# Cross-attention and FFN, one core: the add of head outputs and residual moves from VectorE to GpSimd

## The reference

```
q, k = layernorm(x), context
scores = (q k^T / 8 + hop products(q, rpe[hops])) * decay(gates)     # causal
h      = scores v / (normalizer + 1e-6)
hn     = headwise_layernorm(h) * (1 + ln_w) + ln_b
x1     = x + hn                                                      # the sum that is moved
n      = layernorm(x1)
out    = x1 + n base_w^T + base_b + 2 * (top-2 router mix of n lora_A) lora_B
```

## The kernel before, in words

| table | steps of t = 0, 1, 2, 3 | what is done |
|---|---|---|
| `SCALE` | 1, 4, 7, 10 | POOL: x_res += ln_b (L670), att_w = att * head_rs (L675), att_w *= 1 + ln_w (L680) |
| `LAYER` | 2, 5, 8, 11 | DVE: x1 = att_w + x_res (L1140), bn_stats (L1143), bn_aggr (L1146) |
| `TURN` | 3, 6, 9, 12 | ACT: rstd (L701, L703); DVE: norm (L1115); PE: transposes (L1225); POOL: x1_b = x1 + base_b (L665) |
| `ROUTE` | 4, 7, 10, 13 | PE: L1357; DVE: the router, twelve small instructions from L1077 to L1102 (`mix`) |
| `BASE` | 5, 8, 11, 14 | PE: transpose of mix (L1330), base product (L1344, L1346) |
| `OUT` | 6, 9, 12, 15 | DVE: out = x1_b + product (L1062); SPq: store |

## Time and profile before

### The profile page before, as it was taken

How to read it: one execution, slowest core, us unless ns; L and a number is a source line. 1 busy time by engine, 2 the same in 40 slices (tenths; PEclk the granted TensorE clock), 3 DMA queues, 4 the chain that set the end, 5 groups by cost and what they waited for, 6 DMA issues and landing times.

```text
span 4462.6 us, 82557 instructions
## 1 busy us (share of the span) xinstructions
PE 3690.6 (83%) x21556; PEld 2143.2 (48%) x21556; DVE 2695.9 (60%) x5561; ACT 1925.9 (43%) x4449; POOL 2188.5 (49%) x2567
## 2 busy tenths in 40 slices
PE   6777878878777877688889888888888888988897
PEld 4555544444444444345445444444444444544443
DVE  4545444444344444377777777777676776777774
ACT  3544444444344434354444444444444444444442
POOL 4567667777677777233333333333333333333332
PEclk9999989999999999799999999999999999999999
DMA  7889989999899999554344344444444434444341
GB/s 219 271 263 304 301 275 313 314 312 313 269 311 316 312 312 313 205 175 143 129 161 151 140 141 134 161 144 137 152 135 157 143 127 162 138 156 135 130 154 47
DMA packets 400329, 912.17 MB, mean 204 GB/s; under 512 B 54234, under 2 KB 152538, under 8 KB 391924
## 3 DMA queue, kind: packets, MB, share of 16 engines
q1 hardware_dynamic: 297716, 574.59, 37.5%
q0 software_dynamic: 102400, 335.63, 23.9%
HBM read 708.17 MB, written 201.85 MB: 204 GB/s over the span
## 4 chain that ended last, share of the span: by engine, by line
PE 31%; DVE 17%; issue 7%; ACT 2%; DVEq 1%; DMA 1%; ACTq 0%; SPq 0%; POOL 0%
PE psum L1344 7%; PE psum L1280 5%; PE psum L1288 5%; PE psum L1225 4%; PE psum L1304 3%; PE psum L1258 3%; DVE arena L1011 2%; PE psum L1346 2%; DVE arena L1019 1%; PE psum L1357 1%; DVE arena L1087 1%; DVE arena L991 1%; DVE arena L1082 1%; DVE arena L998 1%; DVE arena L1021 1%
## 5 line engine op out<-in xcount | busy, mean ns | idle before, releaser
L634 POOL DMA_INDIRECT arena<-in_L_xattn_rpe_dram,arena x1280 | 1220.0, 953 | 512.1 <-issue 305.7
L1200 PE MATMUL psum<-arena 128*128 128x128 f32 x5120 | 743.2, 287 | 350.2 <-DMA arena<-in_L_xattn_rpe_dram,arena 169.0
L1200 PEld LDWEIGHTS psum<-arena 128*128 128x128 f32 x5120 | 564.8, 145 | 632.7 <-DVE arena L471 241.3
L471 DVE COPY arena<-psum 128x512 f32<-128x512 f32 x640 | 442.6, 692 | 399.3 <-PE psum L1200 395.9
L471 ACT COPY arena<-psum 128x512 f32<-128x512 f32 x640 | 376.2, 588 | 644.2 <-PE psum L1200 643.8
L1211 PE MATMUL psum<-arena 128*64 128x128 f32 (+3 forms) x4096 | 649.3, 449 | 2.9 <-DVE arena L471 2.2
L654 POOL TENSOR_SCALAR_AFFINE_SELECT arena<-arena 128x256 f32<-128x256 f32 x256 | 113.4, 443 | 1033.2 <-ACT arena L779 1029.7
L479 DVE COPY arena<-psum 128x128 f32<-128x128 f32 (+3 forms) x512 | 251.3, 491 | 536.6 <-PE psum L1211 530.3
L1225 PE MATMUL psum<-arena 128*128 128x128 f32 x2176 | 346.6, 294 | 241.9 <-ACT arena L756 118.5
L779 ACT ACTIVATE arena<-arena 128x512 f32<-128x512 f32 (+3 forms) x1024 | 503.7, 557 | 54.3 <-issue 51.2
L1011 DVE TENSOR_TENSOR arena<-psum,arena 128x1024 f32<-128x1024 f32 (+1 forms) x384 | 400.6, 1043 | 183.9 <-PE psum L1288 159.0
(11 more groups left out here) (100 smaller groups left out, 4427.6 us busy)
## 6 DMA issues: line engine op xcount, KB each, us to landing
hop_products<-arena SPq DMA_DIRECT2D x64, 1024.0 KB, 6.2
arena<-in_x_dram SPq DMA_DIRECT2D x256, 256.0 KB, 4.0
arena<-gate_rows SPq DMA_DIRECT2D x128, 512.0 KB, 3.8
arena<-hop_products SPq DMA_DIRECT2D x128, 512.0 KB, 5.6
hop_products<-arena SPq DMA_DIRECT2D x64, 768.0 KB, 5.4
arena<-hop_products SPq DMA_DIRECT2D x128, 384.0 KB, 4.4
arena<-in_x_dram SPq DMA_DIRECT2D x512, 64.0 KB
hop_products<-arena SPq DMA_DIRECT2D x64, 512.0 KB, 4.7
```

The lines of the kernel that those rows point to most:

```text
L471: copy(rowsT[v % 2][:, :, o[2] * P:(o[2] + 1) * P], bank(1 + n % 2).rearrange("p (k m) -> p k m", k=KT)).then_inc(stage.sem, stage.step(o))
L634: nc.gpsimd.indirect_dma_start(out=rows[v][:, t, :], out_offset=None, in_=rpe[:, :], in_offset=bass.IndirectOffsetOnAxis(ap=here[:, t, v:v ...
L1200: last = nc.tensor.transpose(bank(1 + n % 2)[:, q * P:(q + 1) * P], rows[v][:, o[2], q * P:(q + 1) * P], ident)
```

## The change

The add `x1 = att_w + x_res` is taken from DVE's `LAYER` step and put on POOL behind the scaling of the same tile, one step earlier. The waits that spoke of DVE's x1 now speak of POOL's; DVE's bn_stats waits for POOL's x1. POOL's new instruction waits for its own L680 and for the norm (L1115) of two tiles before, which reads the same buffer of x1.

```diff
@@ steps of the semaphores @@
             for t in at_step(LAYER, s):
-                dve_f_steps[part] += [(n, t) for n in ("x1", "stats", "mean")]
+                dve_f_steps[part] += [(n, t) for n in ("stats", "mean")]
             for t in at_step(SCALE, s):
-                pool_f_steps[part] += [(n, t) for n in ("x_b", "scale", "weight")]
+                pool_f_steps[part] += [(n, t) for n in ("x_b", "scale", "weight", "x1")]
@@ SyncE, load_residual @@
-                sp.wait_ge(*dve_f.at(r.b, ("x1", (t - 2) % ST), 1 if t < 2 else 0))
+                sp.wait_ge(*pool_f.at(r.b, ("x1", (t - 2) % ST), 1 if t < 2 else 0))
@@ GpSimd, x1_b @@
-                        pool.wait_ge(*dve_f.at(r.b, ("x1", t)))
+                        pool.wait_ge(*pool_f.at(r.b, ("x1", t)))
@@ GpSimd, SCALE @@
-                            pool.wait_ge(*dve_f.at(rf.b, ("x1", (t - 1) % ST), 1 if t < 1 else 0))
+                            pool.wait_ge(*pool_f.at(rf.b, ("x1", (t - 1) % ST), 1 if t < 1 else 0))
...
                             nc.gpsimd.tensor_tensor(flat, flat, ln_w1, ALU.mult).then_inc(*pool_f.inc(("weight", t)))
+                            pool.wait_ge(*pool_f.at(rf.b, ("weight", t)))
+                            pool.wait_ge(*dve_f.at(rf.b, ("norm", (t - 2) % ST), 1 if t < 2 else 0))
+                            nc.gpsimd.tensor_tensor(x1[t % 2], flat, x_res[t % 2], ALU.add).then_inc(
+                                *pool_f.inc(("x1", t)))
@@ VectorE, LAYER @@
-                        dve.wait_ge(*pool_f.at(r.b, ("weight", t)))
-                        dve.wait_ge(*pool_f.at(r.b, ("x1_b", (t - 2) % ST), 1 if t < 2 else 0))
-                        nc.vector.tensor_tensor(x1[i], att_w.rearrange("p h d -> p (h d)"), x_res[i],
-                                                ALU.add).then_inc(*dve_f.inc(("x1", t)))
-                        dve.wait_ge(*dve_f.at(r.b, ("x1", t)))
+                        dve.wait_ge(*pool_f.at(r.b, ("x1", t)))
                         nc.vector.bn_stats(f_stats[:, 0:6], x1[i]).then_inc(*dve_f.inc(("stats", t)))
```

## The result

The changed kernel takes 4551.91 us (median of 4 runs, 4543.33 to 4565.5), the one before 4463.36 (4 runs); the ratio is 1.0192 (95% interval 1.0166 to 1.0218). Forecast were 4511 us and a range up to 4548: the direction was right, the size was not. The profiled executions have spans of 4462.6 and 4541.6 us, 79 us apart, all of it in the second stage; the medians are 88.5 us apart, and the profiled execution is the fastest of the four of the changed kernel, which range over 22 us. In many of the executions further down, of the kernel before too, the first stage took 2312 to 2376 us instead of 1819, so their whole times lie near 5000 us.

The account below looks back on a forecast made before the run. The second stage was taken as bound mostly by PE, crossing to DVE at the router of steps 4 and 7 and step 8's add. 37.8 - 25.6 + 23.3 + 11.2 = +46.7 us gave 4511 us, range 4464 to 4548.

Parts of the forecast that it names:

- the add leaves DVE in step 8: Step 8: L1143 starts 0.71 us earlier in some 36 batches, -25.6 us; no more, since elsewhere PE is late.
- step 10 (and 1): Step 10: the add delays DVE's L1082, 0.40 us unhidden in 28 batches, +11.2 us; step 1 taken as nothing.
- router in steps 4 and 7: DVE's L1095 is caught behind the new GpSimd add, 64 collisions of 0.59 us, +37.8 us.
- x1_b of tile 2 loose: Step 8: L665, no longer waiting for DVE's add, gets in before L1001 and delays it, 31 x 0.75 = +23.3 us.
- the rival's meeting: Router: the add starts 0.07 us behind L680 and meets L1090 instead of L1095, +0.90 us each, 4531 us; chance 0.20.
- the clock that the prediction kept "for the range": Idle times of step 8 cut up anew could change the clock by some tens of us; not in the sum.
- step 1 at nothing: Step 1: the add lengthens L1087 by 0.6 to 0.8 us off the chain; nothing taken, at most 6 us.
- the masks: Step 7: the mask starts 1.46 us after L680, the add ends 1.26 us after it, so masks are not late.
- the clock behind L1330: Steps 5 and 8: PE's longer pause, 1.63 us, lowers the clock, 62 times 1.6 us = 99 us, 4610 us; chance 0.05.
- rival of 0.90 per meeting: Router: the add comes level with L1090 instead of catching L1095, 0.90 instead of 0.59 us each, 4531 us; chance 0.20.
- faster case: Router and step 8: DVE keeps the port lock, nothing is added and 25.6 us are gained, 4439 us; chance 0.10.
- about 40% of the 64: Threshold for a faster kernel: fewer than this share of router collisions come about and L665 stays behind L1001.

Follow-up runs that it names:

- e3: Changed kernel with the GpSimd add waiting for the router's mix at all tiles and x1_b held until bn_stats: ratio 0.9917, second stage 2609.1 us.
- e10: Changed kernel with x1_b held until bn_stats and the add waiting for the router's mix only for tiles 1 and 2: ratio 0.9937, second stage 2619.1 us.
- e1: Changed kernel with x1_b held back until DVE's bn_stats of the same tile: ratio 1.0053, second stage 2681.1 us.
- e11: Changed kernel with 8 unused floats placed between x_res and att_w: 4560 us in one run, the add still 1.27 us.
- e16: Changed kernel with 2 unused floats between x_res and att_w, moving att_w and x1 but not x_res: 4547 us in one run, add 1.09 us.
- e2: Changed kernel with the GpSimd add waiting for the router's mix at all tiles, x1_b left loose: ratio 0.9997, second stage 2647.1 us.
- e6: No add on either engine (head outputs left out of x1), x1_b held until bn_stats: ratio 0.9892, second stage 2604.1 us.
- e9: Changed kernel with the add waiting for the router's mix only for tiles 1 and 2, x1_b not held: ratio 0.9998, second stage 2656.4 us.
- e14: Changed kernel with the wait on the norm moved ahead of L680, leaving one wait before the add: ratio 1.0200, second stage 2730.0 us.
- e8: Kernel before, add still on DVE, with only the scaling of tiles 1 and 2 one step earlier (steps 3 and 6): ratio 0.9856, second stage 2575.4 us.
- e15: Changed kernel with 2 unused floats placed before x_res, so it and all behind start at multiples of 32 bytes: 4601.55 us, ratio 1.0297.
- e5: Kernel before, add left on DVE, plus an extra 128x512 GpSimd memset behind the scaling: ratio 1.0022, second stage 2687.0 us.

## Why the prediction was wrong

The terms of its sum against the second stage of four kernels that differ by one step each, from before to changed. The last two columns split the measured time into PE's pauses and the time in which PE is busy:

| term | predicted | kernels | measured | PE's pauses | PE busy |
|---|---|---|---|---|---|
| the add leaves DVE in step 8 | -25.6 | e3 - before | -34.5 | -23.1 | -11.4 |
| step 10 (and 1) | +11.2 | e10 - e3 | +10.0 | +22.0 | -12.0 |
| router in steps 4 and 7 | +37.8 | e1 - e10 | +62.0 | +46.4 | +15.6 |
| x1_b of tile 2 loose | +23.3 | changed - e1 | +41.4 | +19.3 | +22.1 |
| sum | +46.7 | | +78.9 | +64.6 | +14.3 |

All four mechanisms are there, each with its sign. Each row is the difference of two single profiles and is uncertain by 3 to 10 us. Every term of the prediction is a pause, so the pauses are what it is to be held against; there the router and step 10 were sized too small and the other two about right. PE's busy time was put at nothing in the sum. It goes up and down with the time at the lower clock, which is 359 us in the second stage of the kernel before, 301 in e3, 284 in e10, 308 in e1 and 390 in the changed kernel; that the clock is all of it is not shown.

*Router: "the add runs from 3021.08 to 3022.17".* This is the step that failed. The start, 0.17 us behind L680, and the victim, L1095 (now L1100), were right; the duration was taken from L680 "of the same size", and it is 1.27 us: 0.77 instead of 0.59 per meeting. What makes it so is shown by e11 to e16, which change nothing but addresses and order. L1100 is caught in 28 of 32 batches in each of the two steps: 56 x 0.77 = 43 us. Six times L1095 is caught instead, +1.1 us each: 7. In all of the trace that happens 11 times, in batch 0 and the last three, and each time the add starts 0.08 us behind L680 instead of 0.16: the rival's meeting, with the rival's start. PE's waits agree: for the transpose of mix they are 103.0 us in e10 and 155.0 in e1, +52. The last 10 us are PE's busy time, +15.6, less some shorter waits elsewhere.

*x1_b: "31 x 0.75 = +23.3".* The direct term is right: 30 meetings of 0.72 us, 22 us; PE's wait before L1305 grows by 20.6, its pauses by 19.3. The other half, +22.1, is busy time, and it goes with the clock that the prediction kept "for the range": in the body the lower clock lasts 259 us instead of e1's 208, behind step 8 96 instead of 61. Against the kernel before, which has 256 and 96 there, this is no new loss; what e1 had gained is gone again. Nor does the stretch of 6.8 us come from the loose x1_b alone, since e2 has x1_b loose and the stretches of the kernel before. Why the same pause brings one stretch, two or none stays open.

*The gain: "it can't be more".* It was 34.5, and 39.5 in e6. The term itself was right: PE's pauses fell by 23.1 (its waits for the norm and for L756, L762 in e3, by 16 of these). The rest is again PE busy less, with 205 us at the lower clock in e3's body instead of 256 and the pause before L1226 down from 2.2 to 1.5 us.

*Step 10: "28 x 0.40 = +11.2".* That the measured +10.0 comes close is luck. The pauses grew by 22.0, twice the term, and a lower busy time took 12.0 back. In the body PE's wait for the transpose of tile 2 grew from 1.0 us in e3 to 16.7 in e10, 0.58 per batch and not 0.40.

Right were: step 1 at nothing in the body (PE's waits for the transpose of tile 3 sum to 0.0 us in e10's body and 2.4 in e9's), the masks (L654 starts 1.47 us behind L680 as before: 1.46), and L1092, as long as before in steps 4 and 7 (0.91 and 0.88 us on average) and longer in step 1 (1.19 and 0.32); it grew in step 10 as well (0.58 and 0.31). Of the rivals the clock behind L1330 did not come: PE waits 1.78 us there, the clock stays up until 3061.7, and the body has no more of the lower clock than before. The rival of 0.90 per meeting is the 11 cases above and e14. The faster case fell with every caught row; its "about 40% of the 64" does not follow from the prediction's own numbers, by which 21 meetings, a third, already put the time back above 4450. The range was too narrow because it took the meeting's price from two kinds of rows, both with an add of 1.09 us, and left little for the clock, with which single steps moved PE's busy time by 11 to 22 us.

## What to carry to other kernels

Before an elementwise instruction goes to GpSimd, list what DVE runs beside its new place: each dependent two-input instruction there waits for its end, whatever its own size (0.16 us became 0.93), and if PE waits behind that chain it pays in full. Look for a step in which DVE runs none of these, or let the add wait until they are through; and look at what the move sets free behind it, as x1_b here. The same move costs 79 us as it stands, about nothing with a wait for the router (e2), and gains 35 with x1_b held as well (e3); moving what GpSimd already does out of the router's steps (e8) is worth more than the add. Take the duration of a GpSimd instruction from one whose inputs lie the same way, not from one of the same shape.

## What the runs showed of the hardware

- A GpSimd tensor_tensor of 128x512 float32 takes 1.09 us when its two full-size inputs start at different offsets within 32 bytes (0 and 24) and 1.27 when they start at the same one (both 0 or both 24). Moving x_res, att_w, x1, x1_b and what lies behind them by 8 bytes made L670, L680 and L665 0.18 us longer each and the kernel 1% slower (e15). The Trainium skill ("GPSIMD Engine Reference", "Elementwise — side-by-side cycle accounting") puts a two-input tensor_tensor at about 2.6 cycles per element, since the two inputs take turns at the read port; as an estimate that is 1.11 us for 512 elements at its 1.2 GHz. The trace agrees for different offsets, not for equal ones.
- A GpSimd instruction that waits for DVE's scan gets in before the next DVE instruction, 30 times of 32 (L665 in the rows above).
- A memset on GpSimd leaves DVE's two-input instructions alone and still holds a tensor_scalar (e5: 0.83 us on average instead of 0.60).
- Less than 0.1 us in a GpSimd instruction's start decides whom it meets: in all 11 cases in which the changed kernel's add caught L1095 it had started 0.08 us behind L680; where it caught L1100 it had started 0.16 us behind it.
- The granted clock can stay at 1.2 GHz for a second stretch of 3.4 us in which PE never pauses (the second window of the changed kernel).
